# One TensorE gather batch in every 2.8 groups of edges instead of one in every three

## The reference, cut to what matters

```
msg  = relu(x[src] + edge_attr @ We + be)
aggr = segment_sum(msg, dst)
h    = relu(((1 + eps) * x + aggr) @ W1 + b1) @ W2 + b2
h    = relu(batchnorm(h) * gamma + beta) + x
out  = layernorm(x + h)
```

## Time and profile before

| | |
|---|---|
| median of 3 runs | 1575.66 us (1574.07 to 1578.65) |
| the profiled execution | 1577.36 us, span 1575.4 us |
| busy: PE, ACT, POOL, DVE | 90%, 80%, 73%, 57% of the span |
| gathers by GpSimd | 1,145 from xb, 31 from x, 3 for the rest |
| picks and joins on TensorE | 128 batches: 7,168 and 8,064 products |
| mean granted TensorE clock | 0.978 of full speed |

### The profile page before, as it was taken

How to read it: one execution, slowest core, us unless ns; L and a number is a source line. 1 busy time by engine, 2 the same in 40 slices (tenths; PEclk the granted TensorE clock), 3 DMA queues, 4 the chain that set the end, 5 groups by cost and what they waited for, 6 DMA issues and landing times.

```text
span 1575.4 us, 60398 instructions
## 1 busy us (share of the span) xinstructions
PE 1417.6 (90%) x23395; PEld 1094.2 (69%) x23395; DVE 891.4 (57%) x3166; ACT 1259.9 (80%) x3709; POOL 1154.0 (73%) x1193
## 2 busy tenths in 40 slices
PE   1399999999999999999999999999999899999875
PEld 1277777777777777777777777777777677777534
DVE  4775566555566655655555555554555556555336
ACT  0588888888888888888788788787888778888655
POOL 7677777777777777777777777777777777777732
PEclk9999999999999999999999999999999999999987
DMA  9544454455444455445444444444444444444412
GB/s 261 160 108 112 111 121 111 111 119 122 112 112 107 114 120 112 112 113 118 106 113 109 104 112 112 106 111 106 112 106 108 109 105 112 117 112 112 153 27 83
DMA packets 148468, 180.72 MB, mean 115 GB/s; under 512 B 41677, under 2 KB 128932, under 8 KB 147924
## 3 DMA queue, kind: packets, MB, share of 16 engines
q1 hardware_dynamic: 102489, 89.62, 24.4%
q0 software_dynamic: 37728, 77.31, 20.8%
q10 hardware_dynamic: 7963, 9.90, 2.1%
HBM read 170.09 MB, written 6.63 MB: 112 GB/s over the span
## 4 chain that ended last, share of the span: by engine, by line
PE 40%; POOL 34%; issue 12%; DMA 5%; DVE 4%; ACT 3%; SPq 0%; ACTq 0%; POOLq 0%; DVEq 0%
POOL xg L575 34%; PE ps L1341 14%; PE ps L1326 10%; PE ps L1280 7%; PE ps L1266 5%; DMA xg<-xb,idxb 3%; DMA iota_all<-in_x 2%; ACT hot L720 1%; PE ps L1307 1%; ACT msg L726 1%; PE ps L1287 1%; PE ps L1405 1%; PE ps L1395 1%; PE ps L1310 1%; DVE msg L948 1%
## 5 line engine op out<-in xcount | busy, mean ns | idle before, releaser
L575 POOL DMA_INDIRECT xg<-xb,idxb x1145 | 1105.0, 965 | 359.2 <-issue 338.9
L948 DVE TENSOR_TENSOR msg<-ps,xg 128x512 f32<-128x512 f32 x390 | 265.1, 688 | 356.1 <-DMA xg<-xb,idxb 237.4
L689 ACT ACTIVATE iota_all<-ps 128x384 bf16<-128x384 f32 x896 | 379.5, 483 | 39.1 <-PE ps L1326 34.1
L713 ACT ACTIVATE hot<-iota,rel 128x64 f32<-128x64 f32 x1560 | 391.5, 339 | 0.0
L1341 PE MATMUL ps<-iota_all,hot_all 128*128 128x128 bf16 x4032 | 258.8, 220 | 0.0
L1341 PE MATMUL ps<-iota_all 128*128 128x128 bf16 x4032 | 258.5, 220 | 0.0
L1341 PEld LDWEIGHTS ps<-iota_all,hot_all 128*128 128x128 bf16 x4032 | 226.0, 98 | 43.9 <-issue 21.9
L1341 PEld LDWEIGHTS ps<-iota_all 128*128 128x128 bf16 x4032 | 225.7, 98 | 43.3 <-issue 41.0
L726 ACT ACTIVATE msg<-msg 128x512 f32<-128x512 f32 x390 | 241.1, 618 | 18.2 <-DVE msg L948 17.9
L1266 PE MATMUL ps<-we,ea 64*128 64x128 f32 x3126 | 233.0, 289 | 18.3 <-DVE msg L948 17.8
L1280 PE MATMUL ps<-msg,hot 128*64 128x128 f32 x3120 | 222.5, 287 | 23.3 <-ACT msg L726 22.6
(11 more groups left out here) (136 smaller groups left out, 1089.3 us busy)
## 6 DMA issues: line engine op xcount, KB each, us to landing
ea<-in_eat SPq DMA_DIRECT2D x156, 320.0 KB
lowB<-lowD SPq DMA_DIRECT2D x128, 224.0 KB
xg<-xb,idxb POOLq DMA_INDIRECT x1145
accT<-in_xt ACTq DMA_DIRECT2D x1, 3125.0 KB, 14.1
x<-in_xt ACTq DMA_DIRECT2D x1, 3125.0 KB, 11.0
iota_all<-in_x ACTq DMA_DIRECT2D x1, 3080.0 KB, 28.8
out<-iota_all SPq DMA_DIRECT2D x5, 512.0 KB
xb<-iota_all SPq DMA_DIRECT2D x3, 784.0 KB, 10.4
```

The lines of the kernel that those rows point to most:

```text
L575: pool.indirect_dma_start(out=xg[0:rows, slot, j, :], out_offset=None, in_=of, in_offset=bass.IndirectOffsetOnAxis(ap=index, axis=0)).then ...
L689: act.activation(rows3[:, t, :, :].rearrange("p a h -> p (a h)"), ps_rows(k * NTILE + t), ACT.Copy)\
L713: last = act.activation(hot[:, q % TURN, m, :], iota, ACT.Abs, bias=rel[:, t:t + 1], scale=-1.0)
L948: add = dve.tensor_tensor(both, lin_of(half), xg[:, g % RING, :, :].rearrange("p (b t) h -> p b (t h)", b=2), ALU.add)
```

## The change

A batch now belongs to every 2.8 groups: 32 batches to 90 groups, in a pattern that repeats after 45 pairs. The steps are no longer shared out batch by batch but numbered through and spread evenly over the visits, so that a visit can hold the end of one batch and the start of the next; `parts` cuts it there, and the joins of the new batch stand behind the following picks. `NBATCH` becomes 136, the last for group 382. The number of a batch is a plain integer everywhere. `pairs_of` moves from behind `add_window` to behind `ranks`; ScalarE's `take` of visit 2q − 1 moves ahead of `keep_slots`; `slotS` and `lowB` get three buffers; the picks use three banks in turn throughout. The node pair and low number of every looped edge are worked out (1,560 columns), not only those of the batches (390). `lift` and `remains` go over two blocks at a time (`short`) instead of fourteen. Left out below: the same renaming of arguments elsewhere, and the prelude's loops.

```diff
-    RING = ROUND // 2
+    RING = 15
...
-    SORTED = (2, 5, 8, 11, 14, 17, 20, 23, 26, 29)
-    NB = len(SORTED)
...
-    NSTEP = NB * NTILE
     VISITS = 2 * STEPS
-    FIRST = tuple(3 * k - 3 for k in range(NB))
-    SHARE = tuple((3, 2, 2) if k % 2 else (2, 3, 2) for k in range(NB))
-    K0 = 0
+    PER, OVER = 32, 90
+    SKIP = 0
...
-    CYCLE = 3 * GROUP
-    K1 = 7
...
-    VISIT = [[] for _ in range(VISITS)]
-    for k in range(NB):
-        t = 0
-        for d, count in enumerate(SHARE[k]):
-            VISIT[(FIRST[k] + d) % VISITS] += [(-((FIRST[k] + d) // VISITS), k, t + e) for e in range(count)]
-            t += count
-        assert t == NTILE
-
...
+
+    def visit_of(b, t):
+
+        return ((b + SKIP) * NTILE + t) * OVER // (PER * NTILE) - 3
+
+    def group_of(b):
+
+        return visit_of(b, NTILE - 1) + 3
+
+    NBATCH = next(b for b in range(LOOPED) if group_of(b) > 383)
+    BATCH_OF = {group_of(b): b for b in range(NBATCH)}
+    VISIT = {}
+    for b in range(NBATCH):
+        for t in range(NTILE):
+            VISIT.setdefault(visit_of(b, t), []).append((b, t))
+    assert len(BATCH_OF) == NBATCH and visit_of(0, 0) // 2 - 4 >= -PRELUDE
+
+    def set_of(b):
+        return b % 2
...
-        slotS = sb("slotS", [P, 2, EDGES], f16)
+        slotS = sb("slotS", [P, 3, EDGES], f16)
...
-        lowB = sb("lowB", [P, 2, NPAIR * CAP], f16)
+        lowB = sb("lowB", [P, 3, NPAIR * CAP], f16)
...
-        NCOL = NB * ITERS * HALF
+        NCOL = LOOPED * GROUP
...
 
-            return g in SORTED and live(i, SORTED.index(g))
...
-            return batch(j, k) * NTILE + t
+            return i * ROUND + g in BATCH_OF
...
         def phase(i, q, ahead):
 
-            found = []
-            for k in range(NB):
-                turn, step = divmod(FIRST[k] // 2 - ahead, STEPS) if q >= 0 else (0, FIRST[k] // 2 - ahead)
-                if step == q:
-                    found.append((i - turn, k))
-            return [(j, k) for j, k in found if live(j, k)]
+            return [b for b in range(NBATCH) if visit_of(b, 0) // 2 - ahead == i * STEPS + q]
 
         def visit(i, v):
 
-            if v < 0:
-                i, v = i - 1, v + VISITS
-            return [(i + turn, k, t) for turn, k, t in VISIT[v] if live(i + turn, k)]
+            return VISIT.get(i * VISITS + v, [])
...
+            return [b for b, t in visit(i, v) if t == NTILE - 1]
+
+        def parts(i, v):
+
+            steps = visit(i, v)
+            cut = next((m for m, (b, t) in enumerate(steps) if t == 0 and m), len(steps))
+            return steps[:cut], steps[cut:]
+
+        def by_pool(n):
+
+            return GROUP - HALF * (n in BATCH_OF)
...
+        def parts(i, v):
+
+            steps = visit(i, v)
+            cut = next((m for m, (b, t) in enumerate(steps) if t == 0 and m), len(steps))
+            return steps[:cut], steps[cut:]
...
-            def keep_slots(j, k):
-
...
+            def keep_slots(b):
...
                 act.activation(lowS[:, :], low_at, ACT.Copy).then_inc(s_low, 1)
-                old = prior(j, k)
-                if old is not None:
-                    act.wait_ge(s_sel2, old + 1)
-                act.activation(slotS[:, set_of(k), :], slot_at, ACT.Copy).then_inc(s_slotS, 1)
-
...
+                if b >= 3:
+                    act.wait_ge(s_sel2, b - 2)
+                act.activation(slotS[:, b % 3, :], slot_at, ACT.Copy).then_inc(s_slotS, 1)
...
-                    for j, k, t in visit(i, 2 * q):
-                        keep_rows(j, k, t)
-                    for j, k in phase(i, q, 3):
-                        keep_slots(j, k)
-                    for j, k in ending(i, 2 * q - 1):
-                        take(j, k)
+                    for b, t in visit(i, 2 * q):
+                        keep_rows(b, t)
+                    for b in ending(i, 2 * q - 1):
+                        take(b)
+                    for b in phase(i, q, 3):
+                        keep_slots(b)
...
-                source = ps[:, 3:7, :].rearrange("p a n -> p (a n)")[:, 0:LOOPED * GROUP]\
-                    .rearrange("p (m c) -> p m c", c=CYCLE)[:, :, CYCLE - HALF:CYCLE]
+                source = ps[:, 3:7, :].rearrange("p a n -> p (a n)")[:, 0:NCOL]
                 step(dve.tensor_scalar(near, source, 0.5 - SUB, 1.0 / pair, ALU.add, ALU.mult))
...
+            def pairs_of(b):
+
+                c0 = first_tile(b)
...
-            def select_nodes(j, k):
-
...
+            def select_nodes(b):
+
+                old = prior(b)
                 dve.wait_ge(s_lowB, 16 * (b + 1))
                 if old is not None:
                     dve.wait_ge(s_st1, old * NTILE + NTILE)
...
+            def select_edges(b):
+
+                old = prior(b)
                 dve.wait_ge(s_slotS, b + 1)
                 if old is not None:
                     dve.wait_ge(s_join, old * NTILE + NTILE)
...
+            def short(a, b):
+
+                return [(c, min(c + 2, b)) for c in range(a, b, 2)]
...
-                dve.tensor_tensor(xrow[0:SUB, a:b, :], xrow[0:SUB, a:b, :],
-                                  beb[0:SUB, :].unsqueeze(1).to_broadcast([SUB, b - a, HID]), ALU.add).then_inc(s_lifted, 1)
+                for c, d in short(a, b):
+                    last = dve.tensor_tensor(xrow[0:SUB, c:d, :], xrow[0:SUB, c:d, :],
+                                             beb[0:SUB, :].unsqueeze(1).to_broadcast([SUB, d - c, HID]), ALU.add)
+                last.then_inc(s_lifted, 1)
...
+                for c, d in short(a, b):
+                    to = xrow[0:SUB, c:d, :] if which == 0 else x3[0:SUB, c:d, 2, :]
+                    last = dve.tensor_tensor(to, xrow[0:SUB, c:d, :], x3[0:SUB, c:d, which, :], ALU.subtract)
+                last.then_inc(s_rest[which], 1)
...
-                    for j, k in phase(i, q, 3):
-                        ranks(j, k)
+                    for b in phase(i, q, 3):
+                        ranks(b)
+                    for b in phase(i, q, 4):
+                        pairs_of(b)
                     add_x(i, 2 * q, n)
-                    for j, k in phase(i, q, 1):
-                        select_nodes(j, k)
+                    for b in phase(i, q, 1):
+                        select_nodes(b)
                     add_x(i, 2 * q + 1, n + 1)
...
-                    for j, k in phase(i, q, 4):
-                        pairs_of(j, k)
-                    for j, k in phase(i, q, 1):
-                        select_edges(j, k)
+                    for b in phase(i, q, 1):
+                        select_edges(b)
...
-            def pick(j, k, t):
-
...
+            def pick(b, t):
+
...
-                old = n - distance(ring_of, p, NSTEP)
-                if not isinstance(old, int) or old >= 0:
-                    pe.wait_ge(s_rows, old + 1)
+                if n >= 3:
+                    pe.wait_ge(s_rows, n - 2)
...
-                    for j, k, t in visit(i, 2 * q):
-                        pick(j, k, t)
-                    for j, k in phase(i, q, 3):
-                        place(j, k)
-                    for j, k, t in visit(i, 2 * q - 1):
-                        join(j, k, t)
+                    for b, t in parts(i, 2 * q - 2)[1]:
+                        join(b, t)
+                    for b, t in visit(i, 2 * q):
+                        pick(b, t)
+                    for b in phase(i, q, 3):
+                        place(b)
+                    old, new = parts(i, 2 * q - 1)
+                    for b, t in old:
+                        join(b, t)
...
-                    for j, k, t in visit(i, 2 * q + 1):
-                        pick(j, k, t)
-                    for j, k, t in visit(i, 2 * q):
-                        join(j, k, t)
-                    for j, k in phase(i, q, 4):
-                        count(j, k)
+                    for b, t in visit(i, 2 * q + 1):
+                        pick(b, t)
+                    for b, t in new:
+                        join(b, t)
+                    for b, t in parts(i, 2 * q)[0]:
+                        join(b, t)
+                    for b in phase(i, q, 4):
+                        count(b)
```

More of the change, by code:

```diff
@@ L223, in gine_layer_kernel @@
         src_f = hot_all[:, 4224:4224 + (TBLK + 1) * P].rearrange("p (b e) -> p b e", e=P)
-        assert 512 + 2 * NCOL <= FULL + 1 and 2560 + (TBLK + 1) * P <= 4224 and 4224 + (TBLK + 1) * P <= N and 0 < TREST
-        assert all(g % 3 == 2 for g in SORTED) and ROUND % 3 == 0
+        assert 3 * NCOL <= N and 2560 + (TBLK + 1) * P <= 4224 and 4224 + (TBLK + 1) * P <= N and 0 < TREST
         SEL1 = NPAIR * 2 * CAP
@@ L412, in run, with gathered @@
+        def by_pool(n):
+            return GROUP - HALF * (n in BATCH_OF)
+        def gathered(n):
+            return 16 * sum(by_pool(m) for m in range(n % RING, n + 1, RING))
         def run(eng, iteration):
@@ L587, in iteration @@
                             pool.wait_ge(s_xb[q], stores(q))
```

(28 more changed lines are left out.)

189 lines of the change are left out of this document (81 added, 108 removed).

## The result

The changed kernel took 1579.23 us (median of 20 runs, 1576.39 to 1581.88) beside 1576.43 of the kernel before (20 runs, 1572.88 to 1579.32): ratio 1.0018, 95% interval 1.0012 to 1.0025. That is within 0.3% and so inside the range, but it went up where the forecast of 1572.4 went down. The profiled execution took 1578.27 us, its span is 1576.5.

A forecast was written before the change was run, and what follows sets the result against it. The gathers ended the kernel before; TensorE would end the changed one. Pair 190's window 3.0 us earlier and 0.3 for the late gather took 3.3 off 1577.36, to 1574.1; less the profiled execution's 1.7 offset, 1572.4 us, range 1556 to 1590.

The forecast's parts named there:

- The bound: Whole run: the end passes from GpSimd's gathers (7.43 us a pair after the change) to TensorE (7.34 us a pair).
- TensorE's work and its waits for ScalarE: Per 45 pairs on TensorE: work 324.9 us plus waits of 5.2 in 15 pairs, together 330.1, or 7.34 a pair.
- the list: Every pair of a 45-pair period, with ScalarE's path set against TensorE's to find each wait; 15 of 45 wait.
- The pair with 1.02: One pair per period with placing, three joins, the take, then the slots: 7.40 against 6.38, a wait of 1.02 us.
- New joins come first after a window: TensorE, nine pairs a period: joins wait for the previous batch's take, 0.02 to 0.13 us each, 2.5 over the run.
- From the execution to the median: Profiled execution lies 1.7 us above the median of runs shown, 1575.66, so 1574.1 becomes a forecast of 1572.4.
- The start: VectorE's lifting and splitting of x, cut into short pieces: TensorE's first window comes 2.4 us later, bounds 0 and 5.2.
- the 11 us of the estimate: Start on VectorE: by the skill page's 150 cycles, 72 more instructions would cost an estimated 11 us.
- At nothing: Effects counted as zero, chiefly comparing node pairs earlier, which removes TensorE waits (48 us, 24 places) in the gathers' half.
- keep the end: Rival, chance 0.15: without TensorE's waits for ScalarE, gathers still end the run at 1548, or 1560 with half gone.
- the rival named: VectorE late, chance 0.17: in 50 of 136 batches matrices wait for joins; beyond some 0.25 us margin, 1585 or 1598.
- its whole fixed part: Rival, chance 0.06: the start's 72 more instructions cost 11.2 us instead of 2.4, giving 1581.

The follow-up runs named there:

- run 4: The changed kernel with 31 batches in 90 groups (132 over the run) instead of 32: 1561.92 us, ratio 0.9918 to the kernel before.
- run 5: The changed kernel with 30 batches in 90 groups (128 over the run), all other edits kept: 1584.56 us, ratio 1.0027 to the kernel before.
- run 6: The changed kernel with 33 batches in 90 groups (140 over the run): 1612.03 us, ratio 1.0199 to the kernel before.
- run 7: The changed kernel with 63 batches in 180 groups (134) and new joins behind their step's picks: 1559.45 us, ratio 0.9875.
- run 12: The changed kernel (136 batches) with new joins behind the picks, slots ahead of the take, and the start's pieces uncut: 1566.59 us, ratio 0.9946.
- run 1: The changed kernel with new joins that stood first behind a window put behind that step's picks: 1569.85 us, ratio 0.9975 to the kernel before.
- run 11: The changed kernel (136 batches) with new joins behind the picks and the start's pieces uncut: 1569.32 us, ratio 0.9968.
- run 3: The changed kernel with the start's lifts and remainders whole again (24 instructions, not 96): 1576.69 us, ratio 1.0019 to the kernel before.
- run 8: The changed kernel with node pairs compared behind the adds into the sums again: 1578.91 us, ratio 0.9992 to the kernel before.
- the three edits: New joins behind the picks, slots ahead of the take, start's pieces uncut; on the changed kernel with 134 batches: 1554.89 us, ratio 0.9874.
- run 9: The changed kernel unaltered, beside the kernel before on one more chip: 1579.29 us against 1575.19, ratio 1.0029.
- run 13: The kernel before, unaltered, profiled once more: that execution took 1575.09 us, the median of ten was 1579.59.
- run 14: The changed kernel with 30 batches in 90 groups (128) and the start's pieces uncut: 1580.46 us, ratio 1.0000 to the kernel before.
- run 10: The changed kernel with 63 batches in 180 groups (134), new joins behind the picks, slots ahead of the take, start's pieces uncut: 1554.89 us, ratio 0.9874.

## Why the prediction was wrong

- **The bound** (right). GpSimd loses its place in the chain, the last gather is 25 us earlier, TensorE is busy 92% at a granted clock of nine tenths and more in the page's row until the end, and VectorE's wait for gathers is gone. Runs 4 to 7 show both lines and their crossing.
- **TensorE's work and its waits for ScalarE** (right). 36 of 45 pairs agree with the list to 0.02 us. The pair with 1.02, the take ahead of the slots, is there; run 12 takes 0.44 of it away.
- **The step that failed: "New joins come first after a window in nine pairs of a period and wait for the previous batch's take, 0.02 to 0.13 each: 2.5 over the run."** The pairs and the place were right, the size was not: 1.66 a period, 6.9 us over the run by the changed kernel's own trace, 7.5 by run 1. The sum gives no working for its 0.02 to 0.13. By the trace the start is 0.08 late with one join and 0.18 with two, because 0.14 to 0.15 us pass between the end of the releasing copy and the matmul, and the 0.08 by which the first join holds longer there stands nowhere in the sum. The term is 4.4 us too small (6.9 less 2.5), and the sum missed the profiled execution by 4.2 (1574.1 against 1578.27). This turns the sign: with 4.4 more, the forecast's −3.3 for the profiled execution is +1.1, and +0.9 was measured (1578.27 against 1577.36).
- **From the execution to the median** (wrong). The forecast took off 1.7 us because the profiled execution lay that far above three runs. Over 20 runs that execution lies 0.93 above the median, and the changed kernel's 0.96 below its own, so the subtraction put the forecast 2.7 us too low (1.7 less −0.96). Both misses together are the 6.8 from 1572.4 to 1579.2.
- **The start** (right by its stretch, not settled by the time). From the first lift to the first comparison of nodes eight profiles with the cut have 32.0 to 32.4 us, five without it 29.8 to 30.1, so the cut costs about 2.2. The first windows are 1.6 apart in the mean (85.8 to 87.9 and 83.5 to 85.8) and scatter with the landing of x, behind which the first lift starts at 34.1 to 36.5. How much of it reaches the median where TensorE sets the end lies between 0.5 (runs 1 and 11) and 2.5 us (run 3). The 28 short lifts take 9.48 us against 7.83, 0.07 for each instruction more. The Trainium skill's fixed cost ("VectorE: DVE Perf Modes", TRN2 errata) is there, half hidden as the forecast had it, and not the 11 us of the estimate.
- **At nothing** (right). Comparing pairs first changes a period by 0.1 us (run 8). One reading was off: of the 47.9 us of waits for node pairs, 13.1 in two places lie in the first 120 us, not in the half that follows the gathers.
- **The rivals.** The gathers do not keep the end with 136 batches. VectorE's edge matrices do wait for joins, 57.6 us in 49 places for the 50 that the rival named; yet TensorE's placing waits for the rank matrix in three places alone, all in the start (24.2 us), and behind it only weight loads wait, 13 times, at most 0.3; so the margin of some 0.25 us held for the products. The start did not cost its whole fixed part.

Why the change brings nothing: it lets the two engines change places. With 30 in 90 (run 5) TensorE's period, before the gathers hold it up, is 324.0, so (331.4 − 324.0) × 4.2 = 31 us shorter over the run: by this estimate TensorE alone would end near 1548 where the gathers end at some 1577. In the order of the kernel before the period is 317.3, which by the same estimate puts TensorE's own end near 1520: the change spends that whole lead. The 14.1 us from 317.3 to 331.4 are what the forecast's prices give for two batches (2 × 6.86 less two seams of 0.1, 13.5); run 5's 324.0 holds the longer wait shown there. Eight more batches take an estimated 30.4 us from the gathers, to about 1547, and bring TensorE to 1579. Six more, with the three edits, give 1554.89.

## What to carry to other kernels

When work is moved from one engine to another, draw both engines' ends over the amount moved and stop at the crossing; the far side can cost all that was gained. In a step-by-step sum, a wait that is nearly covered is not its overhang alone: add the hand-over from the releasing engine, read from a row where that pair of engines meets, times the number of places. Set a single profiled execution against as many runs as there are before correcting for its offset; here the correction was as large as the effect.

## What the hardware showed that I had not expected

The kernel before, which the gathers end, had medians of 1574.5, 1575.2, 1576.4, 1579.9 and 1580.3 us in five sets of runs, the last two on the same chip; the changed kernel, which TensorE ends, had 1579.2 and 1579.3 in two. So the ratio of two kernels with different bounds went from 0.9992 (run 8, nearly the changed kernel) to 1.0029 (run 9) while one side stood still. The gathers' mean busy time was 961 to 976 ns in these profiles; 1,145 of them make 15 ns 17 us. But the profiles do not show that the chips differ in it: 961 to 969 ns in runs 1, 3 and 4, 963 to 976 in runs 5 to 8, 13 and 14, 964 to 969 in runs 9 to 12, each group on a chip of its own. Where the scatter comes from stays open.
